# Decoder kernel: the second batch's tokens on GpSimd's queue, its projections in two banks, the first gate made beside the second

## What is computed

```
xz = einsum('bld,ed->ble', x, in_proj_w)           # x: 8 x 256 x 256
x_in, z = split(xz, 2)                             # 512 channels each
u = silu(causal_conv(x_in, conv_w, 4 taps) + conv_b)
dt, B, C = split(einsum('bld,ed->ble', u, x_proj_w))
delta = softplus(einsum('blr,dr->bld', dt, dt_proj_w) + dt_proj_b)
h = h * exp(delta * A) + (delta * u) * B           # scanned over 256 tokens, 16 states a channel
y = einsum(h, C) + u * D
out = einsum('ble,...', y * silu(z), out_proj_w)
x = layernorm(x + out); then attention, layernorms, experts
```

## Time and profile before

| | us |
|---|---|
| three runs | 1087.57, 1090.51, 1091.41 |
| median | 1090.51 |
| the profiled execution, whole | 1088.32 |
| its span in the trace | 1086.6 |
| front, up to the last address scatters | 0 to about 735 |
| experts and combining | about 735 to 1086.6 |
| busy: PE, DVE, ACT, POOL | 894.2, 818.2, 634.7, 746.1 |

### The profile page before, as it was taken

How to read it: one execution, slowest core, us unless ns; L and a number is a source line. 1 busy time by engine, 2 the same in 40 slices (tenths; PEclk the granted TensorE clock), 3 DMA queues, 4 the chain that set the end, 5 groups by cost and what they waited for, 6 DMA issues and landing times. The chain is left out here.

```text
span 1086.6 us, 17810 instructions
## 1 busy us (share of the span) xinstructions
PE 894.2 (82%) x5032; PEld 740.4 (68%) x5032; DVE 818.2 (75%) x1595; ACT 634.7 (58%) x1580; POOL 746.1 (69%) x648
## 2 busy tenths in 40 slices
PE   6587878898999988988968969707989989998386
PEld 4366657686777777776866757606878877787264
DVE  0569899899999999999999975664655555565276
ACT  4866696785876876966955543404545555555200
POOL 1445575757679889989989985564777777777500
PEclk9698999999999999999988999957999999999889
DMA  7563764745115224224152021439998998898496
GB/s 245 175 210 130 218 219 131 259 140 175 42 37 180 79 65 153 73 105 137 39 159 89 38 73 65 161 133 305 327 300 247 305 288 291 283 295 246 154 365 259
DMA packets 118253, 195.48 MB, mean 180 GB/s; under 512 B 17477, under 2 KB 83171, under 8 KB 115715
## 3 DMA queue, kind: packets, MB, share of 16 engines
q1 hardware_dynamic: 79682, 134.54, 38.8%
q0 software_dynamic: 16512, 35.19, 8.8%
q10 hardware_dynamic: 21952, 24.51, 7.0%
HBM read 155.21 MB, written 75.64 MB: 212 GB/s over the span
## 5 line engine op out<-in xcount | busy, mean ns | idle before, releaser
L466 POOL TENSOR_TENSOR inf_all<-bc_all,du 128x1024 f32<-128x1024 f32 x128 | 300.2, 2362 | 96.2 <-DVEq L1728 48.9
L1730 DVE TENSOR_TENSOR_SCAN DA<-DA,inf_all 128x1024 f32<-128x1024 f32 x128 | 293.2, 2291 | 24.6 <-ACT DA L732 18.9
L2276 POOL DMA_INDIRECT yp_dram<-u,sz x216 | 212.8, 985 | 76.4 <-issue 46.3
L732 ACT ACTIVATE DA<-dl,a_neg 128x255 f32<-128x255 f32 x512 | 212.0, 462 | 0.2
L2343 ACT ACTIVATE u<-DA,sz 128x256 f32<-128x256 f32 x216 | 102.3, 474 | 114.7 <-DMA yp_dram<-u,sz 85.3
L1737 DVE TENSOR_TENSOR hb_all<-DA,bc_all 128x1024 f32<-128x1024 f32 x128 | 156.0, 1219 | 8.3 <-DVE DA L1730 0.5
L2311 PE MATMUL DA<-hb_all,sz 128*128 128x256 f32 x432 | 136.2, 397 | 19.4 <-ACT sz L2336 18.7
L2304 PE MATMUL DA<-sz,hb_all 128*128 128x128 f32 x864 | 133.2, 277 | 2.6 <-issue 2.6
L1154 PE MATMUL Y<-ident,hb_all 128*128 128x128 f32 x1024 | 133.2, 279 | 0.9 <-DVE hb_all L1737 0.8
L1154 PEld LDWEIGHTS Y<-ident,hb_all 128*128 128x128 f32 x1024 | 121.2, 145 | 8.9 <-DVE hb_all L1737 2.3
L2304 PEld LDWEIGHTS DA<-sz,hb_all 128*128 128x128 f32 x864 | 114.8, 194 | 3.0 <-issue 3.0
(11 more groups left out here) (481 smaller groups left out, 1668.4 us busy)
## 6 DMA issues: line engine op xcount, KB each, us to landing
hb_all<-in_w_moe SPq DMA_DIRECT2D x216, 256.0 KB
bc_all<-bc_dram SPq DMA_DIRECT2D x32, 1024.0 KB, 5.8
inf_all<-xe_dram SPq DMA_DIRECT2D x216, 140.0 KB
bc_all<-yp_dram SPq DMA_DIRECT2D x16, 1024.0 KB, 6.4
xe_dram<-zeros ACTq DMA_DIRECT2D x2, 7420.0 KB, 25.8
xe_dram<-zeros ACTq DMA_DIRECT2D x1, 7560.0 KB, 27.1
yp_dram<-u,sz POOLq DMA_INDIRECT x216
xt<-in_xT SPq DMA_DIRECT2D x8, 256.0 KB, 5.9
```

Source lines behind the costliest of these rows:

```text
L466: g.tensor_tensor(inf[(b * NTAU + t) % NI][:, :, :], bc[gr][:, 0, :, :], du[p][:, c, :].unsqueeze(1).to_broadcast([P, SG, T]), ALU.mult).t ...
L732: ins = s.activation(da[:, n, 1:T], dl[p][:, c, 1:T], ACT.Exp, scale=a_neg[:, c, st:st + 1])
L1730: v.tensor_tensor_scan(da[:, :], da[:, :], inf[(b * NTAU + t) % NI][:, :, :].rearrange("p n t -> p (n t)"), 0.0, ALU.mult, ALU.add).then_i ...
L2276: g.indirect_dma_start(yp_dram, bass.IndirectOffsetOnAxis(ap=pid[:, half * UNROLL + s_:half * UNROLL + s_ + 1], axis=0), ys[s_][:, :], Non ...
```

## The change

There are three parts.

1. The token load of batch 1 is taken out of SP's order and issued by GpSimd, between its set-up and its first inflow. It waits for the same event as before (`proj_f` at 9) and counts on a semaphore of its own, `xt1_in`.
2. Batch 1's projections use PB for f = 0 and QA for f = 1 (`proj_bank`), for the input projection, the convolution and z. PE then waits for the copy of the group two before, not of the group just before. The second group of the input projection waits for nothing.
3. In ACT, `x_in(1, 0)` moves to between decays 0 and 1 of batch 0, and `x_in(1, 1)` to behind decay 1. Silu of `sz0` goes from there to turn 0, directly ahead of the two Silus of batch 1 (`first_gate`).

```diff
+        def proj_bank(b, f):
+            return QA if b == 1 and f % 2 == 1 else PB
@@ SP
             def x_load(b):
                 if proj_f.at(b - 1, 6, True):
-                    sp.wait_ge(proj_f.sem, proj_f.at(b - 1, 9 if b == 1 else 6))
+                    sp.wait_ge(proj_f.sem, proj_f.at(b - 1, 6))
@@ SP turn
-                if s == -1:
-                    x_load(1)
@@ POOL, ahead of the turns
+            pool.wait_ge(proj_f.sem, proj_f.at(0, 9))
+            pool.sem_inc(tick, 1)
+            g.dma_start(xt[:, :, :], a["xT"][:, :, bass.ts(1, T)]).then_inc(xt1_in.sem, 16)
@@ ACT: x_in, conv_out and z_in read proj_bank(b, f) in place of PB
-                s.activation(xin[:, 2 * f:2 * f + 2, TAPS - 1:], pair(PB), ACT.Copy).then_inc(proj_c.sem, 1)
+                s.activation(xin[:, 2 * f:2 * f + 2, TAPS - 1:], pair(proj_bank(b, f)), ACT.Copy).then_inc(proj_c.sem, 1)
@@ ACT first_batch
                 decay(0, 0, 0)
+                x_in(1, 0)
                 decay(0, 0, 1)
-                act.wait_ge(proj_c.sem, 8)
-                s.activation(sz[0][:, :, :], sz[0][:, :, :], ACT.Silu).then_inc(gate_d.sem, 1)
+                x_in(1, 1)
+            def first_gate():
+                act.wait_ge(proj_c.sem, 8)
+                s.activation(sz[0][:, :, :], sz[0][:, :, :], ACT.Silu).then_inc(gate_d.sem, 1)
@@ ACT turn
                     z_in(s + 1, 1 - p, 1)
+                    if s == 0:
+                        first_gate()
                     gates(s + 1, 1 - p)
-                if exists(s + 2) and s > -2:
+                if exists(s + 2) and s > -1:
                     x_in(s + 2, 0)
@@ PE in_proj
+                elif b == 1:
+                    if f > 1:
+                        pe.wait_ge(proj_c.sem, proj_c.at(1, f + 1))
                 else:
                     pe.wait_ge(proj_c.sem, proj_c.at(b, f if f < 2 else f + 2))
@@ PE conv_
-                pe.wait_ge(proj_c.sem, proj_c.at(b, f + 2))
+                pe.wait_ge(proj_c.sem, proj_c.at(b, f + (1 if b == 1 else 2)))
```

More of the change, by code:

```diff
@@ L154, in decoder_kernel @@
         k_pool = sig("k_pool")
-        xt_in = sig("xt_in", 16)
+        xt_in, xt1_in = sig("xt_in", 16), sig("xt1_in", 16)
         proj_f = sig("proj_f", 9)
@@ L673, in conv_out @@
                     c = 2 * f + i
-                    ins = s.activation(du[p][:, c, :], pair(PB)[:, i, :], ACT.Identity, bias=b_conv[:, c:c + 1])
+                    ins = s.activation(du[p][:, c, :], pair(proj_bank(b, f))[:, i, :], ACT.Identity, bias=b_conv[:, c:c + 1])
                 ins.then_inc(proj_c.sem, 1)
@@ L680, in z_in @@
                 act.wait_ge(proj_f.sem, proj_f.at(b, f + 5))
-                s.activation(sz[p][:, 2 * f:2 * f + 2, :], pair(PB), ACT.Copy).then_inc(proj_c.sem, 1)
+                s.activation(sz[p][:, 2 * f:2 * f + 2, :], pair(proj_bank(b, f)), ACT.Copy).then_inc(proj_c.sem, 1)
             def gates(b, p):
@@ L1095, in in_proj @@
                 if f == 0:
-                    pe.wait_ge(xt_in.sem, xt_in.at(b, 16))
+                    if b == 1:
+                        pe.wait_ge(xt1_in.sem, 16)
+                    else:
+                        pe.wait_ge(xt_in.sem, xt_in.at(b - 1, 16))
                 if f == 0:
@@ L1102, in in_proj @@
                         pe.wait_ge(proj_c.sem, proj_c.at(b - 1, 8))
+                elif b == 1:
+                    if f > 1:
+                        pe.wait_ge(proj_c.sem, proj_c.at(1, f + 1))
                 else:
                     pe.wait_ge(proj_c.sem, proj_c.at(b, f if f < 2 else f + 2))
+                bank = proj_bank(b, f)
                 if f < 2:
@@ L1108, in in_proj @@
                         for k in range(KD):
-                            ins = mm(pair(PB)[:, i, :], w_in[:, k, c * P:(c + 1) * P], xt[:, k, :],
+                            ins = mm(pair(bank)[:, i, :], w_in[:, k, c * P:(c + 1) * P], xt[:, k, :],
                                      start=k == 0, stop=k == KD - 1)
@@ L1112, in in_proj @@
                     for k in range(KD):
-                        ins = mm(PB[:, :], xt[:, k, rows_half(f - 2)], w_in[:, k, DI:], start=k == 0, stop=k == KD - 1)
+                        ins = mm(bank[:, :], xt[:, k, rows_half(f - 2)], w_in[:, k, DI:], start=k == 0, stop=k == KD - 1)
                 ins.then_inc(proj_f.sem, 1)
             def conv_(b, f):
-                pe.wait_ge(proj_c.sem, proj_c.at(b, f + 2))
+                pe.wait_ge(proj_c.sem, proj_c.at(b, f + (1 if b == 1 else 2)))
                 for i in range(2):
@@ L1120, in conv_ @@
                     for k in range(TAPS):
-                        ins = mm(pair(PB)[:, i, :], w_tap[:, c * TAPS + k, :], xin[:, c, k:k + T], start=k == 0, stop=k == TAPS - 1)
+                        ins = mm(pair(proj_bank(b, f))[:, i, :], w_tap[:, c * TAPS + k, :], xin[:, c, k:k + T], start=k == 0, stop=k == TAPS - 1)
                 ins.then_inc(proj_f.sem, 1)
```

## The result

The changed kernel takes **1082.0 us**, the median of 5 runs from 1080.19 to 1086.31; the kernel before takes 1090.51, the median of 5 from 1087.57 to 1092.41. The medians differ by 8.5 us. The ratio of the two groups of runs is 0.993, with a 95% interval from 0.991 to 0.996, and that is 7.5 us less, between 4.9 and 10.1. The forecast was 1083.2. The same program timed a second time, with a larger group of runs of before, gave 1081.75 against 1089.7, a ratio of 0.993 (0.990 to 0.995).

The account below looks back on a forecast made before the run. DVE's scans were taken to bound the front. Landing 3.1 + banks 4.0 + clock 1.2 - Silu 1.0 = 7.3 us, so 1090.51 - 7.3 = 1083.2 us, range 1080 to 1089.5.

Parts of the forecast that it names:

- What bounds the front: DVE's scans set the pace in the front: DVE is busy 69.76 of 72 us from 248 to 320 us.
- the measuring point: Start of the scan of tile 6, 75.19 us before, forecast about 67.9; behind it DVE has hardly a gap.
- Rival (b): In turns 0 and 1 half the gain is lost, by a DMA or PE's clock; 1087 us; chance 0.12.
- The landing: Batch 1's tokens land at 40.0 us on GpSimd's queue instead of 43.1: 3.1 us gained, bounds 1.5 and 5.4.
- Rival (a): Queues share the DMA engines, so tokens land at 43.1 as before; gain 4.2 us at most, 1086.4 us; chance 0.20.
- The two banks: PE's four waits for ACT to empty PB, 1.47, 0.69, 0.93 and 0.93 us, go: 4.0 us gained.
- The clock: PE's second input projection group for batch 1 takes 2.6 us instead of 3.77: 1.2 us gained, bounds 1.8 and -0.7.
- ACT's order: Silu of `sz0` ahead of decay 6 costs 1.0 us; sooner decays 2 and 3 give nothing of their own at scan 6.
- The hole: DVE's idle time of 8.03 us ahead of the scan of tile 4 shrinks to about 0.9 us.
- The bound of 8.0 us: At scan 6 no more than 8.0 us can be gained, since decay 5 and then the gates hold ACT.
- rival (c): Token load lands much later and holds the scans; 1096.5 us with landing at 53; chance 0.06, half a real loss.
- the formula: For a late token landing L the gain is 4.0 - (L - 43.1) us, gone at L = 47.1.

Follow-up runs that it names:

- the own buffer: Changed kernel, but SP loads batch 1's tokens at the very start, with no wait, into a buffer of their own; ratio 0.994 to the kernel before.
- The late load: Changed kernel, but GpSimd's token load also waits for the operand of its first inflow, issued at 40.28 us; ratio 0.996 to the kernel before.
- the own buffer with the gate at its old place: Changed kernel with batch 1's tokens in a buffer of their own and the first gate's Silu back behind decay 1; ratio 0.995 to the kernel before.

## Why the prediction was right

The forecast of 1083.2 us missed the 1082.0 by 1.2 us, and the mechanism is the forecast one: tokens sooner, PE's chain of groups closed up, the hole in DVE's work gone. That the number is so close is in part luck. At scan 6 the gain was 8.2 us and not 7.3, since the landing term came out 1.0 too small. Against it stand 1.1 to 1.9 us behind the last scan that I hadn't foreseen. Step by step:

- **What bounds the front** was right, and so was the measuring point. Scan 6 gained 8.2 us and the last scan still had 8.1. Rival (b), the gain lost on the way through the turns, is out for this change: 0.1 us was lost there, 0.2 in the second profile.
- **The landing.** The forecast was 6.4 us from the wait's end. From its issue the load took 6.5 us in the changed kernel and 6.9 when profiled again, but GpSimd issues 0.7 us after PE's last projection of batch 0 ends, where SP had taken 0.1, so from the wait's end it was 7.3 and 7.6 us. It landed at 38.2 us and not at 40.0, because that projection had ended at 31.0 and not at 33.5. Of these 2.5 us, 0.8 is that the whole execution ran earlier. The other 1.7 are PE's clock: the first z group of batch 0 took 3.68 us at a granted clock of 0.52 in the profiled execution of before and 1.98 in the one of after. With the load on SP's queue in such an execution the landing is 41.5. Measured from scan 0, SP's landing is 0.13 us before it in the kernel before and 0.20 in the run with the load on SP's queue, GpSimd's 4.25 us (3.87 in the second profile): the term measured 4.1 (3.7) and not 3.1. In the one profile with GpSimd's load and the slow z group (the gate at its old place) it was 1.85 us before scan 0, which makes the term 1.7. So the 3.1 lies between what the two cases give, and that the better one came in both profiles of the changed kernel was luck, not forecast. Rival (a) is out. A landing 4.1 us earlier was worth 2.6 us at scan 6, as the run with SP's queue shows; the forecast had let it through one for one. The sentence of the Trainium skill (DMA: Bandwidth & Descriptors, section "Issuing engines are not separate DMA queues"), that issuing from several engines saves only issue time, is not borne out here: the same load took 6.5 us on one queue and 11.1 behind 4 MB on the other. The trace agrees with the section "Queues, rings and completion order" of the same page of the Trainium skill, by which each DMA engine takes turns between rings that have work: the load got past four larger ones issued before it.
- **The two banks.** Three of the four waits are gone, 3.5 of the 4.0 us. The wait for the copy behind decay 3, which I had called covered by 0.9 us, is there with 0.55 us, since PE came earlier. The run with one bank lost 5.0 us, which is no contradiction: it takes back the waits and, with the gap ahead of the second group, the clock's term too, 4.0 + 1.2 = 5.2 in the forecast's numbers. From PE's first start on the tokens to `z_in(1, 1)` it took 24.94 us before (43.14 to 68.08) and 19.93 after (38.22 to 58.15), 5.0 us less. So the two terms were right as a pair, and one can't be had without the other.
- **The clock.** The second group took 2.83 us (2.58 in the second profile) against a forecast of 2.6. What I missed is that the low clock can come back at a wait within the chain. It set the size of two of the experiments, at waits of 3.14 and 3.99 us. It doesn't always come: behind waits of 3.15 us (the gate at its old place) and 2.52 (the own buffer) the same z group took 1.98 us, and the granted clock was 1.00. The runs don't show what decides.
- **ACT's order.** From `z_in(1, 1)` to scan 6 it was 7.11 us and became 8.04: the 1.0 us was right. But "they give nothing of their own at the measuring point" was wrong for the kernel as changed. At scan 6 the gate's move is worth 2.1 us more than it costs, and the whole order 4.3 us; at the last scan it is 1.0 and 2.8.
- **The hole.** It vanished instead of shrinking to 0.9 us, and the wait ahead of scan 6 is 2.38 us, forecast 2.4. The bound of 8.0 us was right within 0.2: with the tokens earlier still, scan 6 didn't move.
- **A slower kernel**, rival (c), did not happen. The late load shows its mechanism at work, with scan 1 held by 2.9 us, and the formula gives 3.2 us of gain for a landing at 43.9 where 3.9 were measured.

At scan 6 the three parts are not a sum but a chain. The queue alone gave 0.35 us there and nothing in the device time, with banks and order it gave 2.6 us; the two others without it gave 5.6. Taken out singly they cost 2.6, 5.0 and 4.3 us, 11.8 together, while all three gave 8.2. At the last scan they cost 2.5, 3.2 and 2.8, 8.5 together, against 8.0, so most of that surplus is not seen there; the differences in device time, about 4.0, 4.8 and 4.0 us, are too uncertain to choose.

The 1.1 to 1.9 us that the changed kernel takes longer from the last scan to the first expert go with PE's clock. In the 5 us from the end of the last scan the granted clock was 1.00 in three of the thirteen profiles, and these took 104.5 to 105.0 us to the first expert: the kernel before, one bank, and the own buffer with the gate at its old place. In the other ten it was 0.66, and they took 105.7 to 106.7. The new queue alone, which is no faster than before, is among the ten with 106.2. So the loss is not tied to the gain in the front. No run sets that clock by itself, so the cause stays open.

## What to carry to other kernels

An early transfer is worth only what the next buffer release lets through: before moving a load, find the copy that frees the bank or buffer behind it, and move that too. Before using a profile's event as the start of a forecast, ask whether another execution has it at the same place: here one group of matmuls at the other clock moved it by 1.7 us. A small load that stands behind big ones in one queue can be had sooner on another engine's queue. Price a wait as it will be after the other edits, not as it was before them, and look at what stands ahead of the releasing instruction on its own engine.

## What the runs showed of the hardware

- A load of 256 KB beside 4 MB on SP's queue landed 6.5 to 6.9 us after its issue on GpSimd's queue in five profiles and 7.2 in a sixth, and 8.2 on ACT's; behind the 4 MB on SP's queue it took 9.5 and 11.1, and nearly alone on GpSimd's 3.6. The median landing of the 1 MB loads was 10.1 to 10.5 us beside it, 10.1 with it behind them, and 9.7 to 10.1 without it.
- TensorE's granted clock was 0.50, 1.2 GHz, in the stretch behind a stand of 3.14 us (ACT's old order, from 47.0 on), and a group behind one of 3.99 us (the gate at its old place) was slow in the same way. They took 6.63 us instead of 3.62, and 3.48 instead of 1.98. Behind a stand of 3.15 us in another run the granted clock was 1.00 and the same z group took 1.98.
- The same stretch of code ran at either clock from one execution to the next: the z projection of batch 0, 3.68 us in two profiles, at a granted clock of 0.52 in both, and 1.98 in the eleven others.
- Measured from scan 0, scan 6 repeated to 0.01 us between the two profiles of the changed kernel and the last scan to 0.1 us, while the stage behind the last expert, 43% of whose chain are transfers of one tensor (bc_all<-yp_dram), took 78.5 and 72.7 us.
